# Three-stage attention and expert kernel on one Trainium2 core: table products and their scalings at other places of the pass, norm and slots exchanged at the end of the first stage, the first expert's rows in halves

## The reference

```python
x = _layernorm(x + _L0_attn_ref(x, qkv_weight, proj_weight, proj_bias))   # 32 heads of 8, linear attention
x = _layernorm(x + _L0_ffn_ref(x, router_w, router_b, experts_inter, experts_out))
x = _layernorm(x + _L1_attn_ref(x, W_q, W_k, W_v, b_q, b_k, b_v))
x = _layernorm(x + _L1_ffn_ref(x, gate, corr_bias, w1, w2, fc1_w, fc2_w, up_w, down_w))
```

## Time and profile before

| | |
|---|---|
| median of 3 runs | 2080.05 us (2079.16 to 2084.12) |
| profiled execution | 2083.66 us, span 2081.9 us |
| PE busy | 1879.4 us, 90% of the span |
| DVE busy | 1411.5 us, 68% |
| ACT busy | 874.7 us, 42% |
| GpSimd busy | 750.4 us, 36% |
| mean granted clock of PE | 0.957 |

### The profile page before, as it was taken

The page is one execution under the profiler, slowest core; times in us unless marked ns, Lnnn a source line. Parts: engine busy times, 40 slices in busy tenths (PEclk is TensorE's granted clock), DMA queues, the critical chain, the costliest instruction groups (busy, mean ns, idle before and its releaser), DMA issues.

```text
span 2081.9 us, 35664 instructions
## 1 busy us (share of the span) xinstructions
PE 1879.4 (90%) x11696; PEld 1646.3 (79%) x11728; DVE 1411.5 (68%) x3599; ACT 874.7 (42%) x1623; POOL 750.4 (36%) x774
## 2 busy tenths in 40 slices
PE   7999898549999994999989989989999989989987
PEld 6888787438899993878878878878878878878876
DVE  4777777644444444687787787787787787787666
ACT  3344543423332332444534534544544544544433
POOL 4144553631111105145145145145145145144033
PEclk9999999769999996999999999999999999999999
DMA  3111112132222233012112112112112112211011
GB/s 107 62 61 61 61 61 61 42 122 82 81 81 81 81 102 115 26 52 80 34 52 80 34 52 79 34 52 78 35 53 78 35 53 78 35 53 52 11 41 62
DMA packets 80860, 129.94 MB, mean 62 GB/s; under 512 B 11184, under 2 KB 62000, under 8 KB 80720
## 3 DMA queue, kind: packets, MB, share of 16 engines
q1 hardware_dynamic: 71840, 103.91, 14.9%
q0 software_dynamic: 8880, 24.26, 5.0%
HBM read 103.48 MB, written 24.67 MB: 62 GB/s over the span
## 4 chain that ended last, share of the span: by engine, by line
PE 32%; DVE 15%; issue 7%; ACT 4%; POOL 2%; DVEq 0%; ACTq 0%; DMA 0%; POOLq 0%
PE c_ps L118 7%; PE c_ps L120 6%; PE c_ps L119 6%; PE c_ps L127 3%; PE c_ps L128 2%; PE c_ps L129 2%; PE c_ps L1789 2%; DVE c_shared_place L1706 2%; POOL c_place L1361 2%; DVE c_key L97 1%; DVE c_tmp L97 1%; DVE c_neg_max L1638 1%; DVE c_pre L1548 1%; DVE c_place L1619 1%; PE c_ps L1850 1%
## 5 line engine op out<-in xcount | busy, mean ns | idle before, releaser
L1361 POOL TENSOR_TENSOR c_place<-c_shared_place,c_place 128x512 fp32r<-128x512 f32 x256 | 329.1, 1310 | 376.2 <-DVE c_shared_place L1706 226.6
L1352 POOL DMA_INDIRECT c_gathered<-expert_results,c_slots x112 | 111.8, 998 | 360.5 <-DVE c_pre L1548 340.3
L1706 DVE SCALAR_TENSOR_TENSOR c_shared_place<-c_ps,c_shared_place 128x512 f32<-128x512 f32 x256 | 170.1, 683 | 31.7 <-ACT c_shared_place L1491 30.9
L127 PE MATMUL c_ps<-c_downT_hi,c_place 128*128 128x256 f32 x512 | 150.2, 293 | 16.9 <-POOL c_place L1361 16.9
L118 PE MATMUL c_ps<-c_place 128*128 128x256 f32 (+1 forms) x520 | 149.0, 287 | 17.1 <-DVE c_place L1724 10.0
L1499 ACT ACTIVATE c_place<-c_shared_place 128x512 fp32r<-128x512 f32 x128 | 80.3, 630 | 179.6 <-DVE c_shared_place L1706 178.6
L119 PE MATMUL c_ps<-c_place 128*128 128x256 f32 (+1 forms) x520 | 147.6, 284 | 0.0
L120 PE MATMUL c_ps<-c_place 128*128 128x256 f32 (+1 forms) x520 | 147.5, 284 | 0.0
L1448 ACT ACTIVATE c_shared_place<-c_ps,c_shift_s 128x1024 f32<-128x1024 f32 x64 | 71.4, 1116 | 178.5 <-DVE c_shift_s L1642 164.5
L128 PE MATMUL c_ps<-c_downT_lo,c_place 128*128 128x256 f32 x512 | 142.2, 278 | 0.0
L129 PE MATMUL c_ps<-c_downT_hi,c_place 128*128 128x256 f32 x512 | 142.2, 278 | 0.0
(11 more groups left out here) (373 smaller groups left out, 6101.9 us busy)
## 6 DMA issues: line engine op xcount, KB each, us to landing
c_x2T<-score_rows SPq DMA_DIRECT2D x64, 512.0 KB, 5.5
a_xT_raw<-xT SPq DMA_DIRECT2D x8, 1024.0 KB, 6.6
a_x_rows<-x SPq DMA_DIRECT2D x8, 1024.0 KB, 5.6
x_rows<-a_x SPq DMA_DIRECT2D x8, 1024.0 KB, 4.4
c_pre<-x_rows SPq DMA_DIRECT2D x8, 1024.0 KB
out<-c_x SPq DMA_DIRECT2D x16, 512.0 KB
b_win_raw<-w_in SPq DMA_DIRECT2D x7, 1024.0 KB, 5.5
b_wout_raw<-w_out SPq DMA_DIRECT2D x7, 1024.0 KB
```

Of the source, the lines that this page charges most:

```text
L127: pe.matmul(out, lh, rh, start=False, stop=False)
L1352: pool.indirect_dma_start(rows[:, a, :], None, d["ys"], bass.IndirectOffsetOnAxis(ap=slots[:, a, t:t + 1], axis=0), bounds_check=TRASH + P ...
L1361: pool.tensor_tensor(hid_lo[:, place, :], square[:, place % RING, :], f32(hid_hi[:, place, :]), ALU.subtract).then_inc(hid_split, 1)
L1706: v.scalar_tensor_tensor(square[:, place % RING, :], ps[:, s_bank(unit, k - lag), :], 0.0, factor, ALU.max, ALU.mult).then_inc(s_free, 1)
```

## The change

Four edits.

1. In `ORDER`, `ids` moves from behind `split` to between `proj 1` and `logitT`, and `inv` from behind `proj 3` to between `q 3` and `split`, ahead of `proj 2`.
2. The marks get two semaphores: `columns_marked` when the 16 columns are done, `marked` when the lanes are. ACT's `ids` waits for the first only, PE's `inv` waits for the second and for `ids`.
3. Pass 7 does no `slots`; pass 8 does it for the batch before (`("slots", -1)`) behind its `ln`. So the norm of the last batch comes ahead of `find_slots` of the one before it.
4. The first expert's rows are handled in halves: own semaphore for its first four gathers, then transposes, splits and `hidden` of the first 512 rows, then those of the second. The second expert's gathers are issued when the second half of transposes is done.

```diff
              ("kv", 4), ("x1T", 0), ("kv", 5), ("x1T", 1), ("proj", 0), ("kv", 6), ("kv", 7), ("nd", 3), ("logit", 0), ("logit", 1),
-             ("proj", 1), ("logitT", 0), ("vk", 0), ("vk", 1), ("q", 0), ("q", 1), ("mixT", 1), ("q", 2), ("q", 3),
-             ("split", 0), ("ids", 0), ("proj", 2), ("proj", 3), ("inv", 0), ("slots", 0)]
+             ("proj", 1), ("ids", 0), ("logitT", 0), ("vk", 0), ("vk", 1), ("q", 0), ("q", 1), ("mixT", 1), ("q", 2), ("q", 3), ("inv", 0),
+             ("split", 0), ("proj", 2), ("proj", 3), ("slots", 0)]
...
-            return [unit for unit in ORDER if unit[0] in LATE]
+
+            late = [unit for unit in ORDER if unit[0] in LATE]
+            return [("ln", 0), ("slots", -1)] + late[1:]
...
-        return [unit for unit in ORDER if not (i == 0 and unit[0] in LATE) and not (i == BATCHES - 1 and unit[0] in NEXT)]
+        return [unit for unit in ORDER if not (i == 0 and unit[0] in LATE) and not (i == BATCHES - 1 and unit[0] in NEXT + ("slots",))]
...
             for k in range(PAIRS):
-                eng.tensor_scalar(in_column[:, k, :], counting[:, 0:PLACES], place[:, 0, k:k + 1], None, ALU.is_equal)
+                last = eng.tensor_scalar(in_column[:, k, :], counting[:, 0:PLACES], place[:, 0, k:k + 1], None, ALU.is_equal)
+            last.then_inc(columns_marked, 1)
...
-                        act.wait_ge(marked, i)
+                        act.wait_ge(columns_marked, i)
...
-                        find_slots(i - 1, ps[:, bank_of(i, unit), :], n)
+                        find_slots(i - 1 + j, ps[:, bank_of(i, unit), :], n)
...
                         out = opened(unit)[:, 0:2 * PLACES]
+                        pe.wait_ge(marked, i)
                         pe.wait_ge(ids_done, i)
...
+    FIRST_ROWS = (CH, CH + ICH + CH)
...
-                                            bounds_check=TOKENS - 1, oob_is_err=False).then_inc(xs_in, 16)
+                                            bounds_check=TOKENS - 1, oob_is_err=False).then_inc(first_half_in if e == 0 and t < HTILES else xs_in, 16)
...
-                pool.wait_ge(bank_full, PROLOGUE if e == 1 else group(e - 2, OUT_B))
+                pool.wait_ge(bank_full, FIRST_ROWS[1] if e == 1 else group(e - 2, OUT_B))
...
+                first = isinstance(e, int) and e == 0
+                open_bank = opener(Turns(0, 0, range(BANKS)) if first else turns(e))
+                if first:
+                    turn_rows(e, open_bank, (0,))
                 pe.wait_ge(win_split, e + 1)
 
-                pe.wait_ge(bank_free, PROLOGUE if isinstance(e, int) and e == 0 else group(e - 1, OUT_B))
+                pe.wait_ge(bank_free, FIRST_ROWS[0] if first else group(e - 1, OUT_B))
                 last_a = hidden(e, 0, open_bank)
+                if first:
+                    turn_rows(e, open_bank, (1,))
+                    pe.wait_ge(bank_free, FIRST_ROWS[1])
                 last_b = hidden(e, 1, open_bank)
```

More of the change, by code:

```diff
@@ L229, in number @@
         at = fills(units[:units.index(unit)])
-        if isinstance(i, int) and i < 0:
-            return at
-        if isinstance(i, int) and i == 0:
-            return PROLOGUE + at
-        if isinstance(i, int) and i == BATCHES:
-            return FIRST + (BATCHES - 1) * EACH + at
-        if isinstance(i, int) and i > BATCHES:
-            return FIRST + (BATCHES - 1) * EACH + fills(order(BATCHES)) + at
+        if isinstance(i, int):
+            return sum(fills(order(k)) for k in range(-1, i)) + at
         return PROLOGUE + FIRST + (i - 1) * EACH + at
@@ L954, in split_out, with split_rows @@
                 act.activation(wout_hi[:], wout_raw[:], ACT.Copy).then_inc(wout_hi_done, 1)
-            def split_rows(turn):
+            def split_rows(turn, halves=(0, 1)):
                 for c in range(CH):
-                    for h in range(2):
+                    for h in halves:
                         bank, n = turn.take()
@@ L963, in body @@
             def body(e, end):
-                turn = turns(e)
-                if not (isinstance(e, int) and e == 0):
+                first = isinstance(e, int) and e == 0
+                turn = Turns(0, 0, range(BANKS)) if first else turns(e)
+                if first:
+                    split_rows(turn, (0,))
+                else:
                     act.wait_ge(bank_full, group(e - 1, EACH))
@@ L968, in body @@
                 for h in range(2):
+                    if first and h:
+                        split_rows(turn, (1,))
                     for k in range(ICH):
@@ L984, in _ @@
             split_in(0)
-            split_rows(Turns(0, 0, range(BANKS)))
             body(0, False)
@@ L999, in split_out, with split_rows @@
                 v.tensor_tensor(wout_lo[:], wout_raw[:], f32(wout_hi[:]), ALU.subtract).then_inc(wout_split, 1)
[L1001 to L1006 removed]
+            def split_rows(e, turn, halves=(0, 1)):
+                for j, (c, h) in enumerate((c, h) for c in range(CH) for h in halves):
+                    bank, n = turn.take()
+                    v.wait_ge(xsT_hi_done, 2 * CH * e + CH * halves[0] + j + 1)
+                    v.tensor_tensor(xsT_lo[:, c, bass.ts(h, HALF)], ps[:, bank, :], f32(xsT_hi[:, c, bass.ts(h, HALF)]), ALU.subtract).then_inc(bank_free, 1)
             def store_pairs(e, h, turn):
@@ L1017, in body @@
             def body(e, end):
-                turn = turns(e)
+                first = isinstance(e, int) and e == 0
+                turn = Turns(0, 0, range(BANKS)) if first else turns(e)
+                if first:
+                    split_rows(e, turn, (0,))
                 split_out(e)
                 for h in range(2):
+                    if first and h:
+                        split_rows(e, turn, (1,))
                     for k in range(ICH):
@@ L1037, in _ @@
             split_in(0)
-            split_rows(0, Turns(0, 0, range(BANKS)))
             body(0, False)
@@ L1051, in opener, with turn_rows @@
                 return open_bank
-            def turn_rows(e, open_bank):
-                pe.wait_ge(xs_in, 16 * TILES * e + 16 * TILES)
+            def turn_rows(e, open_bank, halves=(0, 1)):
+                if halves == (0,):
+                    pe.wait_ge(first_half_in, 16 * HTILES)
+                else:
+                    pe.wait_ge(xs_in, 16 * TILES * e + 16 * HTILES)
                 for c in range(CH):
-                    for h in range(2):
+                    for h in halves:
                         out, n = open_bank()
@@ L1093, in _ @@
             pe.wait_ge(ident_done, 2)
-            turn_rows(0, opener(Turns(0, 0, range(BANKS))))
             body(0, False)
```

26 lines of the change are left out of this document (11 added, 15 removed).

## The result

The changed kernel takes 2062.5 us, median of 4 runs (2057.9 to 2064.3), where the kernel before took 2079.6 beside it (2078.8 to 2084.1): a ratio of 0.9907 (0.9889 to 0.9926). 17 us are gained; 33 were forecast. Its profiled execution took 2061.0 us with a span of 2059.3, 22.6 under the span of before. The two gains differ because the profiled execution of before was slower than the median beside it (2083.7 against 2079.6), and that of the changed kernel faster (2061.0 against 2062.5). In later rounds the same kernel gained 22.4 and 23.2 us in the median.

A forecast was written before the change was run, and what follows sets the result against it. TensorE was taken to bound passes 1 to 6, with waits at `inv` and a slow clock; gains of 28.0 us (passes), 4.1 (tail) and 1.2 (halves), together 33.3, gave 2047 us, whole range 2038 to 2060.

The forecast's parts named there:

- The waits at `inv` and the slow clock behind them: Passes 1 to 6: TensorE's 13.9 us of waits and 19.6 us put down to slow clock would go.
- Does a wait of 1.65 us drop the clock? [...] I take that it does not.: Wait before `mixT 0`: clock stays, as behind a 1.52 us wait; otherwise each pass loses 3.9 us again.
- The first rival: Steady passes: waits go but half rate stays, 19.6 us of the gain lost, 2066 us; chance 12%.
- The wait itself: New TensorE wait before `mixT 0`: 1.65 us in passes 2 to 5, 1.35 in pass 6; bounds 0 and 3.2.
- Work per pass: TensorE's work in a full steady pass without waits or slow clock: 41.2 us.
- The tail: Pass 7 to the last `inv`: last `inv` another 4.1 us earlier; bounds 3.2 and 5.4.
- pass 7's start: Pass 7 begins 28.9 us earlier; VectorE's `find_slots` starts 1.4 behind `nd` instead of 0.5, leaving 28.0.
- The halves: First expert's rows in two halves: net gain 1.2 us; bounds 0.5 and 3.0.
- The start of `hidden 0`: First expert: `hidden 0` starts 3.9 us earlier, 2.0 from earlier transposes and 1.8 from half of them moving behind.
- the chain between the halves: Between `hidden 0` and `hidden 1`: 0.9 us of transposes and 1.8 of ACT and VectorE chain, 2.7 given back.
- `ids` never held ACT: Rival, steady passes: late columns make `ids` block ACT; 14 us late costs 41 us, 2088 us; chance 2%.
- the second rival: Head of a pass: VectorE and ACT bound, TensorE waits 3.2 us instead of 1.65, 2055 us; chance 15%.

The follow-up runs named there:

- e1_again: The changed kernel itself, measured again beside the kernel before: 2063.0 us, ratio 0.9893.
- e10_filler_nd2: The changed kernel with eight more products in the first bank of `nd 2`, passes 1 to 6: 2054.8 us, 0.9870 of the kernel before.
- e13_gate_mixT1: Changed kernel with `slots 0` behind `mixT 1`, identity ahead of gathers, GpSimd's `xT` pieces held until `find_slots` ends: 2041.9 us, 0.9782 of before.
- e14_gate_q2: Changed kernel with `slots 0` behind `q 2`, identity ahead of gathers, GpSimd's `xT` pieces held until `find_slots` ends: 2040.8 us, 0.9776 of before.
- e2_order: The kernel before with edits 1 and 2 alone (`ids` and `inv` moved, two semaphores for the marks): 2062.6 us, 0.9880 of before.
- e7_ident_first: The changed kernel with the second stage's identity built ahead of the first expert's eight gathers: 2056.0 us, 0.9882 of the kernel before.
- e9_again: The changed kernel itself, measured again in the third round beside the kernel before: 2056.2 us, ratio 0.9888.

## Why the prediction was wrong

- **The waits at `inv` and the slow clock behind them** went as forecast in kind. The steady pass fell from 47.9 to 43.45 or 45.0 us; 43 was said.
- **The step that failed first: "Does a wait of 1.65 us drop the clock? [...] I take that it does not."** It does, about every second time. From one row with a wait of 1.52 us that kept the clock I took all such waits to keep it. A fall in a pass of the changed kernel costs 1.6 us, not the 3.9 of before. Two such falls in its profile are 3.2 us and four in e1_again 6.4. The first rival had named the mechanism, at a price twice too high and as if it came every time; e10_filler_nd2, e13_gate_mixT1 and e14_gate_q2, without the wait, show it. The profile of before could not have told: it also kept the clock behind the two short waits ahead of pass 1, where 11 of the other 15 profiles lost it. The Trainium skill, page "TensorE: Matmul & The Clock Gate", section "A second HAM failure mode: psum-queue depth-cycling", had the clock go back and forth with small idles. The trace agrees for 17 of 30 such waits, and for the other 13 it doesn't.
- **The wait itself was too small by a mechanism that I hadn't looked for.** 1.65 us were forecast, 2.0 measured in passes 2 to 5 and 1.5 (forecast 1.35) in pass 6: 1.5 us over passes 2 to 6. `find_slots` moved into GpSimd's pieces and grew by 0.53 us, and VectorE's jump took 0.4, not 0.3. That makes 2.3; the 0.3 that the measured wait is shorter isn't traced to a row. The old wait in front of `inv` had kept the two engines apart. The prediction counted what `find_slots` has ahead of it on its own engine and not what runs beside it on another.
- **Work per pass** was 41.45 us (43.45 less the wait), not 41.2: 1.3 over five passes. For e1_again the three make 6.4 + 1.5 + 1.3 = 9.2 of the 9.3 us that its passes gained less than forecast (284.0 - 264.4 = 19.6 against 28.9); for the first profile 3.2 + 1.5 + 1.3 = 6.0 of 6.0.
- **The tail** had 4.1 us less 0.9 of pass 7's start, 3.2; measured 2.8 and 3.2. Right, and by e2_order about 2 us of it hang on edit 3.
- **The halves** had a gain of 1.2 and cost about 1, by the means of a few profiles. The start of `hidden 0` was right (3.7 earlier, 3.9 said), and so was the chain between the halves (2.77 from 444.30 to 447.07; 2.7 said). What I left out is the clock behind `hidden 0`: it stays low for longer there, and the two stretches lose 0.50 of 3.4 and 0.29 of 4.0, 2.9 us, where those of before lost 1.7. And I took the 23.4 us of before from one profile, where two other profiles of the same code have 21.9. e7_ident_first shows the better edit: what held the first half was the identity, which the prediction had seen and did not weigh.
- **The other rivals.** `ids` never held ACT: the exponential followed it at 192.16, directly behind 189.87 + 2.33. The wait of 3.2 us of the second rival did not come; VectorE is the bound at the head of a pass, as it said, but by 2.0 us and through `find_slots` and not through ACT.
- **The sum** was made against one profile that had the early start of pass 1 and the long expert periods. In the first profile after, a start 6.2 us later and expert passes 6.0 us shorter cancel. The first is again the clock behind short waits, ahead of pass 1; what sets the second stayed open. That profile's gain, 22.6 us, misses the forecast 33.3 by 10.7: 6.0 in the passes, 0.4 in the tail, 1.5 in the halves, and a rest of 2.8 in stretches that differ between profiles of one kernel. The measured ratio, 0.9907, lies just outside the stated range, whose upper end of 2060 us is 0.9904 of before, and those of e1_again and e9_again lie just inside: on which side it falls is chance. That 17 to 23 us came where 33 were forecast is not.

## What to carry to other kernels

When a wait goes, look at what other engines do at the moment to which the work behind it moves, and not only at what is queued ahead of it on its own. Price a new wait of 1.5 us on TensorE as the wait and a chance of the clock, and look for an order that has none: here two placements of `slots`, one about level with the changed kernel and one that lost to it, won 0.7% and 1.9% as soon as one wait on GpSimd kept it and VectorE apart. Take a second profile of the same kernel before explaining a difference of 6 us: one profile can't show what happens half of the time.
